# Counts kept as 16-bit integers and turned by the DMA, one-pass row broadcasts, shorter row sums, and a wider weight ring in a fused four-layer graph network

## Time and profile before

| | |
|---|---|
| median of 3 runs | 1565.53 us (1562.76 to 1565.57) |
| the profiled execution's own time | 1563.96 us |
| its span | 1562.2 us |
| TensorE busy, share of the span | 1530.7 us, 98% |
| VectorE, ScalarE, GpSimd | 56%, 48%, 11% |
| granted TensorE clock | 0.998 |

### The profile page before, as it was taken

The page is one execution under the profiler, slowest core; times in us unless marked ns, Lnnn a source line. Parts: engine busy times, 40 slices in busy tenths (PEclk is TensorE's granted clock), DMA queues, the critical chain, the costliest instruction groups (busy, mean ns, idle before and its releaser), DMA issues.

```text
span 1562.2 us, 19437 instructions
## 1 busy us (share of the span) xinstructions
PE 1530.7 (98%) x7082; PEld 1232.1 (79%) x7082; DVE 881.6 (56%) x1403; ACT 754.7 (48%) x1358; POOL 167.1 (11%) x295
## 2 busy tenths in 40 slices
PE   6999999999999999999999999999999999999997
PEld 5877877888887888788778877887888778877775
DVE  8878788787645343322432353667487246434346
ACT  6567666768733333423332233345596236533233
POOL 1100021324300000000000000122021004100003
PEclk9999999999999999999999999999999999999999
DMA  5333153325774434433353335564474248545345
GB/s 193 109 122 117 33 178 115 111 75 184 261 253 157 149 102 145 138 106 123 112 175 121 101 120 169 188 211 167 127 210 157 79 146 285 201 133 170 92 122 179
DMA packets 103329, 231.88 MB, mean 148 GB/s; under 512 B 23168, under 2 KB 26103, under 8 KB 103227
## 3 DMA queue, kind: packets, MB, share of 16 engines
q1 hardware_dynamic: 90126, 191.66, 38.8%
q10 hardware_dynamic: 13100, 38.86, 6.5%
HBM read 171.11 MB, written 59.37 MB: 148 GB/s over the span
## 4 chain that ended last, share of the span: by engine, by line
PE 90%; DVE 4%; ACT 3%; issue 1%; POOL 0%; DMA 0%; ACTq 0%; DVEq 0%; SPq 0%; POOLq 0%
PE bank L945 16%; PE bank L807 15%; PE bank L809 15%; PE bank L808 15%; PE bank L956 9%; PE bank L949 7%; PE bank L947 7%; PE bank L1010 2%; ACT Tt L1091 1%; PE bank L877 1%; DVE Tt L1386 1%; PE bank L970 1%; PE bank L845 1%; DVE oK L1662 1%; ACT Zh L1125 0%
## 5 line engine op out<-in xcount | busy, mean ns | idle before, releaser
L807 PE MATMUL bank<-wh,xh 128*125 128x512 f32 x1032 | 415.5, 403 | 4.4 <-issue 1.5
L808 PE MATMUL bank<-wl,xh 128*125 128x512 f32 x1040 | 410.4, 395 | 0.0
L809 PE MATMUL bank<-wh,xl 128*125 128x512 f32 x1040 | 409.7, 394 | 0.0
L945 PE MATMUL bank<-Zh,Mh 125*125 125x512 f32 x1000 | 399.5, 399 | 1.4 <-ACT Mh L1080 1.4
L1360 DVE TENSOR_TENSOR xl<-xs,xh 128x1000 fp32r<-128x1000 f32 x130 | 155.7, 1199 | 286.4 <-ACT xh L1056 286.1
L1056 ACT CAST xh<-xs 128x1000 fp32r<-128x1000 f32 x130 | 133.4, 1026 | 290.2 <-PE bank L809 273.5
L956 PE MATMUL bank<-Zl,Mh 125*125 125x512 f32 x600 | 236.6, 394 | 0.0
L809 PEld LDWEIGHTS bank<-wh,xl 128*125 128x125 f32 x1040 | 193.0, 186 | 48.9
L807 PEld LDWEIGHTS bank<-wh,xh 128*125 128x125 f32 x1032 | 191.1, 185 | 50.3 <-ACT xh L1056 3.5
L808 PEld LDWEIGHTS bank<-wl,xh 128*125 128x125 f32 x1040 | 193.1, 186 | 44.3
L945 PEld LDWEIGHTS bank<-Zh,Mh 125*125 125x125 f32 x1000 | 185.4, 185 | 45.7 <-ACT Mh L1080 1.8
(11 more groups left out here) (169 smaller groups left out, 1820.4 us busy)
## 6 DMA issues: line engine op xcount, KB each, us to landing
xs<-xT_d SPq DMA_DIRECT2D x80, 500.0 KB, 3.6
Ar<-a_d SPq DMA_DIRECT2D x100, 312.5 KB, 3.2
xs<-hT_d SPq DMA_DIRECT2D x40, 500.0 KB, 3.5
x_d<-XO ACTq DMA_DIRECT2D x30, 512.0 KB, 4.9
R<-x_d SPq DMA_DIRECT2D x60, 256.0 KB, 4.3
xT_d<-XT ACTq DMA_DIRECT2D x30, 500.0 KB, 3.1
ws<-in_W SPq DMA_DIRECT2D x28, 256.0 KB, 3.8
Tt<-m_d SPq DMA_DIRECT2D x10, 625.0 KB, 4.3
```

Source lines behind the costliest of these rows:

```text
L807: te.matmul(o, xh[i % 2][:, k, :], wh[s][:], start=(k == 0), stop=False)
L808: te.matmul(o, xh[i % 2][:, k, :], wl[s][:], start=False, stop=False)
L809: m = te.matmul(o, xl[i % 2][:, k, :], wh[s][:], start=False, stop=(k == 7))
L945: te.matmul(o, Mh[i][:, s, :], zh, start=(n == 0), stop=False)
```

## The change

Nine of the ten count tiles are evicted straight to int16 and turned by one DMA each; their degrees are summed by ScalarE from the turned tile. The last tile keeps the old way. The broadcasts use `transpose` in place of `matmul`. GpSimd folds the row sums down from five blocks to two. The ring of weight staging gets two more places in the `XO` buffers. Some of VectorE's work is reordered.

```diff
-    return (g - 16) % 6 if 16 <= g < 80 else g % 2
+    if g < 72:
+        return g % 8 if g % 8 < 6 else g % 8 + 4
+    return g % 8 % 6 if g < 80 else g % 2
...
+SPLIT_AHEAD = {LAST_X[8] + 1, LAST_X[8] + 2}
...
-    _ring = 6 if 2 <= _h <= 9 else 2
+    _ring = 8 if 2 <= _h <= 8 else 6 if _h == 9 else 2
...
-        AF16 = [sb(f"A16{i}", [128, NT, T], i16, ca) for i in range(2)]
+        AF16 = [sb(f"A16{i}", [128, NT, 128], i16, ca) for i in range(2)]
...
             def store_counts(b):
-                q.wait_ge(s_a16, b + 1)
+                if b < NT - 1:
+                    q.wait_ge(s_ev, 3 * b + 3)
+                else:
+                    q.wait_ge(s_a16, 1)
                 q.wait_ge(d_a[b % 2], 16 * (b // 2))
-                sy.dma_start(a_d[b].rearrange("p (a c) -> p a c", c=T), AF16[b % 2][:]).then_inc(d_a[b % 2], 16)
-                q.wait_ge(s_te, at_group(b, 2) + 1)
+                if b < NT - 1:
+                    q.wait_ge(d_at[b % 2], 16 * (b // 2))
+                    if b >= 2:
+                        q.wait_ge(s_dsum, b - 1)
+                    sy.dma_start_transpose(AT16[b % 2][:], AF16[b % 2][:].rearrange("p a c -> p (a c)")).then_inc(d_turn[b % 2], 16)
+                sy.dma_start(a_d[b].rearrange("p (a c) -> p a c", c=T), AF16[b % 2][:, :, 0:T]).then_inc(d_a[b % 2], 16)
+
+            def store_turned(b):
+                if b < NT - 1:
+                    q.wait_ge(d_turn[b % 2], 16 * (b // 2 + 1))
+                else:
+                    q.wait_ge(s_te, TURNED)
                 q.wait_ge(d_at[b % 2], 16 * (b // 2))
-                sy.dma_start(at_d[b].rearrange("p (a c) -> p a c", c=T), AT16[b % 2][:]).then_inc(d_at[b % 2], 16)
+                sy.dma_start(at_d[b].rearrange("p (a c) -> p a c", c=T), AT16[b % 2][:, :, 0:T]).then_inc(d_at[b % 2], 16)
...
-                te.matmul(bank[b][0:T, 0:T], PQ[0][1][:, d:d + 1].to_broadcast([T, T]), ident[0:T, 0:T],
-                          start=True, stop=True).then_inc(s_tt, 1)
+                te.transpose(bank[b][0:T, 0:T], PQ[0][1][:, d:d + 1].to_broadcast([T, T]), ident[0:T, 0:T]) \
+                    .then_inc(s_tt, 1)
...
-                        for b in range(NT - 1):
-                            for n in range(3):
-                                if c == C_LAST[3 * b + 2] + 4 + 2 * n:
-                                    at_part(b, n)
...
-                for c in range(NT // 2):
+                for c in range(2):
                     m = te.matmul(bank[6 + d % 2][0:T, 0:1], GW[0:T, d % 2, c * T:(c + 1) * T], ones[0:T, 0:1],
...
-                    if t >= 2 and n == 0:
-                        q.wait_ge(s_tt, at_group(t - 2, 2) + 1)
-                        q.wait_ge(s_a16, t - 1)
-                    ac.activation(Af[t % 2][:, :, u:w], bank[b % 4][0:T, 0:NT * (w - u)].rearrange("p (i s) -> p s i", s=NT),
+                    if t >= 2 and n == 0 and t < NT - 1:
+                        q.wait_ge(d_a[t % 2], 16 * (t // 2))
+                        q.wait_ge(d_turn[t % 2], 16 * (t // 2))
+                    q.wait_ge(s_pad, 4)
+                    to = A16[t % 2] if t < NT - 1 else Af[:]
+                    ac.activation(to[:, :, u:w], bank[b % 4][0:T, 0:NT * (w - u)].rearrange("p (i s) -> p s i", s=NT),
                                   ACT.Copy).then_inc(s_ev, 1)
...
+            def degree_sums(t):
+                q.wait_ge(d_turn[t % 2], 16 * (t // 2 + 1))
+                if t:
+                    q.wait_ge(s_dsum, t)
+                ac.activation(AS[:], AT16[t % 2][0:T, :, 0:T], ACT.Copy, accum_out=DEG[:, t:t + 1]).then_inc(s_dsum, 1)
...
-                counts_turned(t)
+                if 1 <= t < NT - 1:
+                    degree_sums(t - 1)
+                elif t == NT - 1:
+                    last_turned()
...
-                        if c == C_LAST[14] + 12:
+                        if c == C_LAST[17] + 12:
                             degrees(0, 5)
...
-                for d in range(5, NT - 1):
+                z_lower(5, 5, G[:, 5, :], DIS)
+                x1_post(NT - 1)
+                for d in range(6, NT - 1):
                     z_lower(d, d, G[:, d, :], DIS)
...
+                for i in FIRST_AT.get(j, []):
+                    if JOBS[i].kind not in ("gate", "att", "kept") and i not in (z0, z1) and i - 3 not in SPLIT_AHEAD:
+                        second(i)
                 if j in LAST_SLABS:
                     for g in SLAB_AT[j]:
                         slab(g)
-                for i in FIRST_AT.get(j, []):
-                    if JOBS[i].kind not in ("gate", "att", "kept") and i not in (z0, z1):
-                        second(i)
...
+                if j in SPLIT_AHEAD:
+                    second(j + 3)
...
-                po.tensor_tensor(s, t[:, 0:5, :], t[:, 5:10, :], ALU.add).then_inc(s_half, 1)
+                chain("p", po.tensor_tensor(s, t[:, 0:5, :], t[:, 5:10, :], ALU.add))
+                mine()
+                chain("p", po.tensor_tensor(s[:, 0:2, :], s[:, 0:2, :], s[:, 2:4, :], ALU.add))
+                mine()
+                po.tensor_tensor(s[:, 0, :], s[:, 0, :], s[:, 4, :], ALU.add).then_inc(s_half, 1)
```

More of the change, by code:

```diff
@@ L285 @@
 ROWS = {7: range(4, 8), 9: range(8, 10)}
-def at_group(b, n):
-    return 3 * b + n + (b == NT - 1)
-ROW_GROUP = 3 * (NT - 1)
+ROW_GROUP = 0
+LAST_GROUPS = (1, 2, 3)
+TURNED = 4
 def tail_groups():
-    of, all_ = {}, [6 + i % 2 for i in range(3 * NT + 1)]
+    of, all_ = {}, [6 + i % 2 for i in range(TURNED)]
     amid = {}
@@ L472, in gnn_program @@
         d_at = [sem(f"d_at{i}") for i in range(2)]
+        d_turn = [sem(f"d_turn{i}") for i in range(2)]
         d_xt = sem("d_xt")
@@ L585, in stage_free @@
                 slab_split(q, o)
+            elif staging(g) > 9:
+                for d in range(NT - 2, NT):
+                    q.wait_ge(s_tt, GROUPS[fin_of(0, d)][-1][0] + 1)
+                    x_stored(q, fin_of(0, d))
             else:
@@ L765, in sync_program @@
                 store_counts(b)
+                if b:
+                    store_turned(b - 1)
                 if b == NT - 3:
@@ L844, in at_part @@
                 for k in range(u, w):
-                    m = te.transpose(bank[6 + i % 2][0:T, (k - u) * T:(k - u + 1) * T], Af[b % 2][:, k, :],
-                                     ident[0:T, 0:T])
+                    m = te.transpose(bank[6 + i % 2][0:T, (k - u) * T:(k - u + 1) * T], Af[:, k, :], ident[0:T, 0:T])
                 m.then_inc(s_tt, 1)
@@ L852, in rows @@
                 for n, d in enumerate(which):
-                    m = te.matmul(bank[b][0:T, n * T:(n + 1) * T], PQ[0][0][:, d:d + 1].to_broadcast([T, T]),
-                                  ident[0:T, 0:T], start=True, stop=True)
+                    m = te.transpose(bank[b][0:T, n * T:(n + 1) * T], PQ[0][0][:, d:d + 1].to_broadcast([T, T]),
+                                     ident[0:T, 0:T])
                 m.then_inc(s_tt, 1)
@@ L967, in row_sums @@
                     q.wait_ge(s_rs, d - 1)
-                q.wait_ge(s_te, 3 * NT + 1 + len(AMID) + sum(1 for o in range(j) for _ in GROUPS[o]))
-                for c in range(NT // 2):
+                q.wait_ge(s_te, TURNED + len(AMID) + sum(1 for o in range(j) for _ in GROUPS[o]))
+                for c in range(2):
                     m = te.matmul(bank[6 + d % 2][0:T, 0:1], GW[0:T, d % 2, c * T:(c + 1) * T], ones[0:T, 0:1],
-                                  start=(c == 0), stop=(c == NT // 2 - 1))
+                                  start=(c == 0), stop=(c == 1))
                 m.then_inc(s_row, 1)
@@ L990, in tail @@
                         col = PQ[(job.layer + 1) % 2][0]
-                        te.matmul(bank[b][0:T, 0:T], col[:, job.d:job.d + 1].to_broadcast([T, T]), ident[0:T, 0:T],
-                                  start=True, stop=True).then_inc(s_tt, 1)
+                        te.transpose(bank[b][0:T, 0:T], col[:, job.d:job.d + 1].to_broadcast([T, T]), ident[0:T, 0:T]) \
+                            .then_inc(s_tt, 1)
                         continue
@@ L997, in tail @@
                         for k in range(4):
-                            m = te.matmul(bank[b][:, k * 128:(k + 1) * 128],
-                                          WC[:, a, 4 * g + k:4 * g + k + 1].to_broadcast([128, 128]), ident[:, :],
-                                          start=True, stop=True)
+                            m = te.transpose(bank[b][:, k * 128:(k + 1) * 128],
+                                             WC[:, a, 4 * g + k:4 * g + k + 1].to_broadcast([128, 128]), ident[:, :])
                         m.then_inc(s_tt, 1)
@@ L1293, in scalar_program @@
                     rows(6 + ROW_GROUP % 2, range(0, 4))
+                    degree_sums(t)
             tanh(J0[0], blocks_of(J0[0], EARLY))
@@ L1487, in post @@
                 if job.kind == "x1":
-                    x1_post(d)
                     z_lower(d, d, G[:, d, :], DIS)
```

75 lines of the change are left out of this document (40 added, 35 removed).

## The result

| | before | after |
|---|---|---|
| median | 1565.05 us (1562.76 to 1565.57, 4 runs) | 1581.44 us (1580.64 to 1582.87, 4 runs) |
| ratio, 95% interval | | 1.0109 (1.0091 to 1.0126) |
| profiled execution, span | 1563.96, 1562.2 | 1581.31, 1579.5 |
| granted TensorE clock | 0.998 | 0.988 |

The forecast was 1543 us, with 1537 to 1554 as its range. The change made the kernel 16 us slower.

What follows compares the result with a forecast made beforehand. TensorE was taken to bound the kernel, with VectorE close behind in the count stage. Savings of 6.5 + 6.0 + 5.5 + 2.5 + 0.3 = 20.8 us from 1563.96 gave 1543 us, range 1537 to 1554.

Steps and rivals of the forecast that it cites:

- The bound: Whole kernel: TensorE, busy 98% of the span; a removed instruction is worth its start-to-start time, except where TensorE waits.
- Part 1: Count stage: 90 transposes and the first broadcast's records removed save 6.5 us, between 0 and 11; the turning DMA stays hidden.
- rival A: Count stage: the turn takes longer than a tile, 12.9 us, so the kernel gets slower, 1582 us; chance 0.07.
- part 5: Between last chunk and first gate product: `x1_post(9)` moves up, the last tile's chain stays; saves 0.3 us.
- Part 2: The other 62 broadcasts, 30 in the gates: one record each by `transpose` in place of two; saves 6.0 us.
- Part 3: Attention row sums: five matmuls become two, with two more GpSimd additions; saves 5.5 us, from -2.5 to 6.5.
- rival D: Attention: VectorE bounds it once GpSimd adds more, part 3 becomes -2.5, 1551.2 us; chance 0.05.
- Part 4: Weight switches: eight slabs staged and reordering at iteration 168 remove TensorE's waits for the features' lower part; saves 2.5 us.
- B: Count stage: VectorE holds it, so part 1 gives nothing, 1549.7 us; chance 0.12.
- C: Broadcasts: one by `transpose` still makes two records; 6.0 and some 0.3 us are lost, 1549.5 us; chance 0.04.
- The two rules: Turning DMA: 1309 ns per block, estimated 13.1 us for ten in sequence, against turning DMAs as fast as regular ones.

Runs made afterwards that it cites:

- e1: The padded kernel: changed kernel with HBM count arrays and loaded tiles padded to 128 columns, so both stores are whole 2560-byte rows; 1539.98 us, ratio 0.984.
- e4: Kernel before with only the 66 broadcasts written as `transpose`; 1560.91 us, ratio 0.9977.
- e5: Kernel before with only the row sums folded to two blocks; 1556.33 us, ratio 0.9938.
- e10: e1 with the ring of six staging tiles and the old order at layer 1's boundary; 1542.74 us, ratio 0.9865.
- e7: e1 with both stores moving 250 of each 256 bytes, HBM pitch still 256 bytes; 1542.26 us, ratio 0.9863.
- e8: e1 with HBM rows at a pitch of 384 bytes, of which whole runs of 256 are written; 1541.92 us, ratio 0.9861.

## Why the prediction was wrong

**The bound.** Right for everything behind the count stage; there the starts of TensorE priced the change.

**Part 1, the count stage: -6.5 forecast, +30.0 measured to the first gate product. This is the step that failed, and in it one sentence:** "SyncE's stores of 250-byte runs (5.1 in place of 2.4 us) have nobody behind them but the store two tiles later." Both halves were wrong.
- The price. I took 5.1 us from a load of the attention, whose 250-byte runs are read out of 2500-byte rows, and this stage's queues were 41% busy. That row couldn't carry it. The 12800 packets of 250 bytes in the kernel before are these loads (1116 to 1182 us); their starts are off 64 bytes just as often, and they take 19.5 ns each, 1.6 us of all queues per DMA. The stores of this change write such runs; they take 59.9 ns each, 9.6 us of all queues per tile. I never made that sum, though the number of runs (1280) and the tile's time (9.3 us) stand in the prediction. I even made it for the turn, under rival A, with 0.108 us a run, where it wasn't needed. The edit has no line that says "other runs": it is `[:, :, 0:T]` on a tile made wider for the turn's sake.
- Who is behind them. The turn of tile b + 1 overwrites the buffer of tile b - 1, whose store is issued behind the turn of tile b. So the next turn waits for a store that is one issue old, and ScalarE and TensorE wait for the turn.

With that price gone (padded kernel) the first gate product comes 10.6 us sooner than before. Part 1 and part 5 said 6.8, with 11 as the most for part 1: VectorE, for which I had taken off a third, rose to 71.11 us busy of 78 and held nothing up. The turn by itself was priced well enough ("I take 5: hidden"): 3.0 to 4.0 us on the median.

**Part 2, broadcasts: -6.0 forecast.** -5.0 in span, 1.9 to 5.5 by the ratio of e4. One record each, as said (L1009 has 30). The forecast lies above both. By records e4 should give 7.2 us, and its trace says where the rest stays: TensorE waits 1.3 us on `XT` (before: none), 2.8 on `xh` (1.4) and 6.4 on the keys (5.8).

**Part 3, row sums: -5.5 forecast, -6.6 measured** between the marks, and 6.5 in e5: all of TensorE's 6.5. The new additions do make VectorE's L1577 longer, as the earlier trace rows let one expect (columns of that group):

```profile
L1577 DVE SCALAR_TENSOR_TENSOR G<-U,R x10: 693/1590/1596, 1169.8 to 1233.3; 125x512 f32<-125x512 f32 x10
```

The median went from 1142 to 1590 ns. But 0.45 us a job was less than the slack: TensorE waited for none of it, and rival D falls.

**Part 4, the switch: -2.5 forecast, 0.8 to 1.6 measured.** The two waits of the earlier trace rows, 2.7 us, are gone. The changed kernel has three that the kernel before has not:

```profile
PE bank L1027 <- ACT XT L1229: 1.2, 1, 1.2
...
PE bank L1027 <- ACT PB L1246: 1.1, 1, 1.1
PE bank L1027 <- ACT XO L1191: 1.0, 1, 1.0
```

The first comes with the broadcasts (e4 has it, and so has e10, without the switch's part). The last two, 2.1 us, lie at the switch. e10 has neither, but 1.6 and 1.3 us of the kind of the earlier trace rows: 2.9 against 2.1 is the 0.8. That the features' lower parts, moved ahead, put `post` back is my reading of the order. I named what goes, not what comes next.

**Part 5: 0.3.** Not told apart from part 1.

**The rivals.** A gave 1582 us, and 1581.4 was measured, but that the numbers meet is luck: its mechanism had the turn taking 12.9 us. Its place (ScalarE stuck on the landing of the turn), its point of decision (10.9 us a tile; 12.7 came) and its sign (the last chunk's end late, then TensorE on its banks) were right; the resource was the queues, filled by the stores, and 0.07 was too little for it. Had I asked of all DMAs of a tile, and not of the new one alone, whether they fit in a tile, A would have had the greater chance. B and C fall: 109.5, and one record each.

**The two rules.** A whole turn landed in 3.0 us on the median, though the queues were full, and in 4.0 in the padded kernel. "VectorE: DVE Perf Modes", section "The three transpose paths", of the Trainium skill gives 1309 ns for a 128x128 block; the estimate of 13.1 us for ten is over three times what either trace shows, so blocks of one DMA don't follow each other at that price. "Advanced Engine Details and Errata", section "X-Bar Transpose (TRN2)", of the Trainium skill has such DMAs as fast as others; in e1 it is near that, if not quite: 4.0 us beside 3.2 and 3.3 for the stores of the same tile.

## What to carry to other kernels

When an edit changes the shape of a tile that a DMA moves, work out again for each DMA of that tile: into how many runs it falls, where in HBM each starts, and runs times price over 16 queues against the time of one step of the loop. Keep runs of a few hundred bytes that are written to HBM on starts of 64 bytes: the same 250-byte runs at a pitch of 256 gave back 39 us (e7), and whole rows with 2.4% more bytes 41 (e1). Take the price of a store from a store: the same runs read cost a third. And where a buffer is used in turn, ask not how many steps apart its uses are, but how long before its next use the last DMA on it was issued.

## What was not expected of the hardware

- **Stores to HBM of 250-byte runs cost by their start.** 19.2 ns a packet with all starts on 64 bytes (pitch 256), 34.9 with one in two off, 48.6 with three in four off, 53.2 to 63.5 with nearly all off. Length and gaps don't do it (e7, e8). Reads show nothing like it: the attention's loads of 250-byte runs take 19.5 ns in the kernel before, 19.2 in the changed one, 18.7 in e7. For reads, "DMA: Bandwidth & Descriptors", section "How a descriptor splits into AXI transactions", of the Trainium skill has a start off 256 bytes fetch from the 256-byte boundary below. By such a rule alone, put to writes, pitches of 320, 288 and 272 bytes, with 3 in 4, 7 in 8 and 15 in 16 starts off 256, would be nearly alike; measured here they gave 1546, 1556 and 1573 us.
- **One thing doesn't fit.** Packets of 2500 bytes in the kernel before start off 64 bytes too (their rows are 2500 bytes apart), and took 108 ns, where 2560-byte rows took 111 (e1; both 40 to 125 us, loads included). So the price is not a fixed sum per odd start; whether it fades with length wasn't tried. Nor is it explained why 252 bytes is slower than 250 and 378.
- **The granted clock is lost with TensorE's work.** 0.91, 0.87 and 0.76 in the three stretches shown, in which it waited for evictions; 1.00 in both stretches of e1. How much of the 30 us it makes was not measured by itself.
